# Attention and expert block on one Trainium2 core: TensorE flips after the probability rows, ScalarE moves rows before it copies operands, sine and cosine move to a head's third step

## The chip, the cores and the metric

The kernel runs on one core of a Trainium2 chip, as one launch. The core has TensorE (PE in the profile; PEld is its weight load), VectorE (DVE), ScalarE (ACT), GpSimd (POOL) and the queue that issues transfers (SP). Each engine works through its own instruction stream in order and waits on semaphores for the others. The metric is the device time of one execution in microseconds (us); lower is better.

## What is computed

A transformer block on x of shape (4, 512, 128), float32, with adaptive layer norms. Its first half is an attention with 16 heads of width 64 and 4 key/value heads. Each token picks 2 of 4 nodes for each head; the rotary angle of a token is its rank among the tokens of the same node, so every head of every batch needs sines and cosines of its own. Its second half is a gated feed-forward with 7 experts, a null expert and a shared one. Cut to what matters here:

```python
for n in range(K_NODES):
    p = pos[..., n]                      # rank of the token in node n, per head
    qr = q * cos[p] + rotate_half(q) * sin[p]
    kr = k * cos[p] + rotate_half(k) * sin[p]
    scores = einsum('bhid,bhjd->bhij', qr, kr) * SCALE
    scores = where(causal & member[..., n], scores, NEG)
    outs.append(einsum('bhij,bhjd->bhid', softmax(scores), v))
y = (weights of the two picked nodes * their outs).sum()
x = x + ga * (y @ wo)
x = x + gb * (top-1 expert + shared expert)(layernorm(x))
```

## The kernel before

The change lies in the attention stage, which takes the span from about 85 us to about 875 us. It runs over 4 batches x 16 heads = 64 heads (`NH`), and in each head over 4 tiles of 128 query rows (`TB`). One tile of one head is a step k = 4n + s, with n the head and s = 0 to 3 the tile; there are 256 steps (`STEPS`). Causality makes a step wider with s: its scores have (s + 1) x 128 columns. Two score matrices (e = 0, 1) are made in each step, one for each picked node.

The order on each engine is written out by hand, as a loop over k in which each engine handles a different, older or newer step:

- TensorE, step k: `scores(k)` (L1092, matmuls on L1102 to L1104 for each of the two matrices), then `flip(k + 2)` (L1079, three transposes on L1087 and L1089 that put rotated queries and keys on end), then `prob_rows(k - 4)` (L1107, s + 1 transposes on L1113 of the weighted probabilities). In an odd head's third step (s = 2) it adds `values` (L1116, 16 matmuls on L1121), in every fourth head's third step `project_value` (L1031), in a fourth step (s = 3) `project(n + 3)` (L1038).
- ScalarE, step k: `keep_qk(k + 1)` (L510, copies a flip from PSUM to `QK`, L513), `move_pt(k - 5)` (L516, copies transposed probabilities from PSUM to `accT` in `arena`, L522, s + 1 blocks wide), `weigh_a(k - 2)` (L538, L543), `exponentials(k)` (L525, two instructions on L534), and in an odd head's third step `keep_y` (L546, L550), which waits for `values`.
- VectorE, step k: `row_max(k)` (L827 or L832), `weigh_b(k - 3)` (L842), `inverse_sums(k - 1)` (L837), in steps s = 0 and 1 the rotary products of head n + 2 (L816), and a piece of the preparation of angles for the next eight heads.
- GpSimd, step k: the rotary sums and the scaled keys of later heads (`rotate`, L390 to L409), then `coefficients(k - 1)` (L416), which need `inverse_sums(k - 1)`.

PSUM has 8 banks. Banks 0 to 3 hold scores; `scores(k)` waits for the exponentials of step k - 2 or k - 3 (`before_use`). Bank 7 (`psM`) serves projections and values. Banks 4 to 6 are shared in turn by flips and probability rows: the list `turns` says in which order the two take them, and `wait_turn` makes the user of a turn wait until ScalarE has emptied the turn three before it. In the order before, a list of turns in mid-stage reads t(k + 1), pt(k - 5), t(k + 2), pt(k - 4): so `flip(k + 2)` waits for `move_pt(k - 6)`, and `prob_rows(k - 4)` waits for `keep_qk(k + 1)`. `scores(k)` waits for `keep_qk(k)`.

Once in eight heads (`SPAN`), `trigonometry` runs on ScalarE: with the two `preload_act_table` calls around it that is a table load (L556), a sine over 128 x 2048 (L504), a cosine over 128 x 2048 (L505) and a table load back (L506). The tables of sines are double buffered; its angles are ready once the preparation on VectorE is done, at the third step of head n % 8 = 4, and its results are first needed by VectorE's products at the first step of head n % 8 = 6. It stands seven times in the stage's loop, in heads 5, 13, ..., 53, all odd.

Of the kernel before, what the change touches and what calls it, by code (L numbers as in the profile page):

```python
# [18 lines left out]
NH = B * H  # L19
STEPS = NH * TB  # L20
HALF = HD // 2
SPAN = 8
# [15 lines left out]
def block_kernel(nc, x, wq, wk, wv, wr, wo, w_router, w_up, w_gate, w_down, ws_up, ws_gate, ws_down,  # L38
                 c, wmod, inv_freq, out):
    ctx = ExitStack()  # L40
    with ctx:
# [180 lines left out]
        def score_area(k, e):  # L222
            b_, w = places(k), (k % TB + 1) * P
            return bank[b_[0]][:, e * w:(e + 1) * w] if len(b_) == 1 else bank[b_[e]][:, 0:w]
# [7 lines left out]

        turns = [("t", 0), ("t", 1)]
        for k in range(STEPS + 2 * TB):
            if k + 2 < STEPS:
                turns.append(("t", k + 2))
            if 0 <= k - 4 < STEPS:
                turns.append(("pt", k - 4))
        turn_of = {what: i for i, what in enumerate(turns)}

        def turn_bank(what):
            return bank[4 + turn_of[what] % 3]

        def wait_turn(eng, what):

            i = turn_of[what] - 3
            if i >= 0:
                eng.wait_ge(S["t_ev" if turns[i][0] == "t" else "pt_ev"], turns[i][1] + 1)
# [213 lines left out]
        def _(act):  # L462
# [25 lines left out]
            def keep_value(g):  # L488
                act.wait_ge(S["v_mm"], g + 1)
                act.activation(v_b[:, g % 3, :, :].rearrange("p t d -> p (t d)"), psM[:, 0:TB * HD], ACT.Copy  # L490
                               ).then_inc(S["v_ev"], 1)
# [8 lines left out]
            def trigonometry(j):  # L500

                sine, cosine = [trig[:, j % 2, i, :, :, :, :].rearrange("p h t s f -> p (h t s f)") for i in range(2)]
                act.wait_ge(S["ang_abs"], 2 * j + 2)
                act.activation(sine, sine, ACT.Sin).then_inc(S["trig_done"], 1)  # L504
                act.activation(cosine, cosine, ACT.Sin, scale=-1.0, bias=half_pi[:, 0:1]).then_inc(S["trig_done"], 1)  # L505
                act.preload_act_table(ACT.Exp)  # L506
# [3 lines left out]
            def keep_qk(i):  # L510
                n, tb = i // TB, i % TB
                act.wait_ge(S["t_done"], i + 1)
                act.activation(QK[:, n % 2, :, tb * P:(tb + 1) * P], turn_bank(("t", i))[:, 0:3 * P].rearrange("p (j t) -> p j t", j=3),  # L513
                               ACT.Copy).then_inc(S["t_ev"], 1)

            def move_pt(k):  # L516
                n, ib = k // TB, k % TB
                w = ib + 1
                act.wait_ge(S["pt_done"], k + 1)
                if n >= 3:  # L520
                    act.wait_ge(S["pv_done"], (n - 3) // 2 + 1)
                act.activation(accT[:, n % 3, 0:w, ib * P:(ib + 1) * P],  # L522
                               turn_bank(("pt", k))[:, 0:w * P].rearrange("p (j i) -> p j i", j=w), ACT.Copy).then_inc(S["pt_ev"], 1)

            def exponentials(k):  # L525
                w = (k % TB + 1) * P
                if k >= 3:
                    act.wait_ge(S["wa_done"], k - 2)
                if k >= 4:
                    act.wait_ge(S["acc_done"], k - 3)  # L530
                for e in range(2):
                    area = score_area(k, e)
                    act.wait_ge(S["negmax_done"], 2 * k + e + 1)
                    act.activation((expB if e else expA)[:, k % (4 if e else 3), 0:w], area, ACT.Exp,  # L534
                                   bias=negmax[k % 4][:, e:e + 1], accum_out=den[k % 4][:, e:e + 1]
                                   ).then_inc(S["exp_done"], 1)

            def weigh_a(k):  # L538
                w = (k % TB + 1) * P
                if k >= 4:  # L540
                    act.wait_ge(S["pt_done"], k - 3)
                act.wait_ge(S["coef_done"], k + 1)
                act.activation(acc[k % 4][:, 0:w], expA[:, k % 3, 0:w], ACT.Copy, scale=coef[k % 4][:, 0:1]  # L543
                               ).then_inc(S["wa_done"], 1)

            def keep_y(p):  # L546
                act.wait_ge(S["pv_done"], p + 1)
                if p >= PAIRS:
                    act.wait_ge(S["wo_mm"], p // PAIRS)
                act.activation(yT[:, p % PAIRS, :], psM[:, :], ACT.Copy).then_inc(S["y_ev"], 1)  # L550

            keep_qk(0)
            for k in range(STEPS + 2 * TB):
                n, s = k // TB, k % TB
                if s == 0 and n % SPAN == 5 and n // SPAN + 1 < NH // SPAN:
                    act.preload_act_table(ACT.Sin)  # L556
                    trigonometry(n // SPAN + 1)
                if k + 1 < STEPS:
                    keep_qk(k + 1)
                if 0 <= k - 5 < STEPS:  # L560
                    move_pt(k - 5)
                if 0 <= k - 2 < STEPS:
                    weigh_a(k - 2)
                if k < STEPS:
                    exponentials(k)
                if s == 2 and n % 2 == 1 and n >= 3:
                    keep_y((n - 3) // 2)
                if s == 2 and n % GROUP == 0 and n // GROUP + 1 < B * KV:
                    keep_value(n // GROUP + 1)
# [428 lines left out]
        def _(pe):  # L998
# [32 lines left out]
            def project_value(g):  # L1031
                b = g // KV
                for tb in range(TB):
                    mm_ = pe.matmul(psM[:, tb * HD:(tb + 1) * HD], hT[:, b * T + tb * P:b * T + (tb + 1) * P],
                                    w_v[:, (g % KV) * HD:(g % KV + 1) * HD], start=True, stop=True)
                mm_.then_inc(S["v_mm"], 1)
# [55 lines left out]
            def scores(k):  # L1092
                n, s = k // TB, k % TB
                u, r, w = n % 2, n % RING, (s + 1) * P
                rows = slice(s * P, w)
                pe.wait_ge(S["t_ev"], k + 1)
                pe.wait_ge(S[f"mm_in{r}"], 16 * (n // RING + 1))
                if before_use[k] is not None:
                    pe.wait_ge(S["exp_done"], 2 * before_use[k] + 2)
                for e in range(2):  # L1100
                    o = score_area(k, e)
                    pe.matmul(o, QK[:, u, e, rows], QK[:, u, 2, 0:w], start=True, stop=False)  # L1102
                    pe.matmul(o, mring[:, r, 1 + e, rows], mring[:, r, 0, 0:w], start=False, stop=False)  # L1103
                    pe.matmul(o[:, s * P:w], identbig[:, :], causal[:, :], start=False, stop=True  # L1104
                              ).then_inc(S["scores_done"], 1)

            def prob_rows(k):  # L1107
                ib = k % TB
                pe.wait_ge(S["acc_done"], k + 1)
                wait_turn(pe, ("pt", k))  # L1110
                psPT = turn_bank(("pt", k))
                for jb in range(ib + 1):
                    mm_ = pe.transpose(psPT[:, jb * P:(jb + 1) * P], acc[k % 4][:, jb * P:(jb + 1) * P], ident[:, :])  # L1113
                mm_.then_inc(S["pt_done"], 1)
# [31 lines left out]
            for k in range(STEPS + 2 * TB):  # L1146
                n, s = k // TB, k % TB
                if k < STEPS:
                    scores(k)
                if k + 2 < STEPS:  # L1150
                    flip(k + 2)
                if 0 <= k - 4 < STEPS:
                    prob_rows(k - 4)
                if k == STEPS + 1:
                    pe.wait_ge(S["exp_done"], 2 * STEPS)
                    last_rows(0, PAIRS - 1)
                if s == 2 and n % 2 == 1 and n >= 3:
                    values((n - 3) // 2)
                if s == 2 and n % GROUP == 0 and n // GROUP + 1 < B * KV:
                    pe.wait_ge(S["prod_done"], 4 * (n + 3))  # L1160
                    project_value(n // GROUP + 1)
                if s == 2 and n % H == 2 and n > H:
                    attention_rows(n // H - 1)
                if s == 3 and n + 3 < NH:
                    pe.wait_ge(S["prod_done"], 4 * (n + 3))
                    if n >= 3:
                        pe.wait_ge(S["y_ev"], (n - 1) // 2)
                    pe.wait_ge(S["v_ev"], min(B * KV, n // GROUP + 2))
                    if n % H == 2 and n > H:
                        pe.wait_ge(S["x1_done"], n // H)  # L1170
                    project(n + 3)
# [176 lines left out]
```

## Time and profile before

| | |
|---|---|
| median of 3 runs | 1094.33 us (1090.01 to 1095.94) |
| profiled execution, its own time | 1083.49 us |
| its span in the profile | 1081.7 us |
| mean granted TensorE clock | 0.933 of full speed |
| busy in the span | PE 901.7 us, PEld 624.1, DVE 777.6, ACT 741.4, POOL 616.7 |
| chain that ended last | PE 53%, DVE 24%, ACT 9%, issue 7%, POOL 5%, DMA 1% |

The profile is of one execution. Engines run beside each other, so their busy times don't add up; where an engine sat idle, the profile names what released it. The chain that ended last says which work the end hung on. Durations and waits are read from the timeline, which lists the instructions in order of their start.

### The profile page before, as it was taken

How to read it: one execution, taken by the hardware profiler on the slowest of the kernel's cores; microseconds unless marked ns; L12 is line 12 of the kernel's file. 1: busy time of each engine (PE TensorE's matmuls, PEld its weight loads, DVE VectorE, ACT ScalarE, POOL GpSimd, SP SyncE). 2: the span in 40 equal slices, each digit the busy share in tenths (PEclk: the TensorE clock that was granted, in tenths of full speed). 3: DMA queues.
4: the chain of work that ended last, by engine and by line, in shares of the span. 5: the costliest groups of instructions: out<-in, count | busy, mean ns of one | idle time of the engine just before them, and what ended most of it. 6: DMA issues, size and time to landing. Idle time of an engine off the chain costs nothing.

```text
span 1081.7 us, 19107 instructions
## 1 busy us (share of the span) xinstructions
PE 901.7 (83%) x5907; PEld 624.1 (58%) x5907; DVE 777.6 (72%) x1577; ACT 741.4 (69%) x2017; POOL 616.7 (57%) x872
## 2 busy tenths in 40 slices
PE   3409979997999799879997997999899999697883
PEld 3406646665676566556764665667566666554552
DVE  6887957995887589957785797687867774565443
ACT  3326778778776877888678778875888886544342
POOL 5118757785775577857775787576756660050232
PEclk9559989998999899989998999999989999699997
DMA  9000000100100010000000001010000004112003
GB/s 212 1 1 7 1 21 22 31 22 11 31 22 21 11 32 22 21 21 22 21 22 21 21 22 32 11 32 11 8 2 2 2 4 173 59 34 62 18 21 95
DMA packets 45602, 32.68 MB, mean 30 GB/s; under 512 B 8032, under 2 KB 43488, under 8 KB 45504
## 3 DMA queue, kind: packets, MB, share of 16 engines
q1 hardware_dynamic: 44288, 28.95, 9.4%
q0 software_dynamic: 1216, 2.51, 0.7%
q8 instruction: 51, 0.84, 0.3%
q14 instruction: 47, 0.39, 0.1%
HBM read 18.30 MB, written 12.36 MB: 28 GB/s over the span
## 4 chain that ended last, share of the span: by engine, by line
PE 53%; DVE 24%; ACT 9%; issue 7%; POOL 5%; DMA 1%; ACTq 0%; DVEq 0%; SPq 0%; POOLq 0%
PE psum L1102 17%; PE psum L1121 7%; DVE pcs L816 5%; PE psum L1113 5%; PE psum L1204 5%; POOL R L390 4%; PE psum L1103 4%; PE psum L1041 4%; ACT probs L534 3%; DVE accs L842 3%; PE psum L1087 3%; DVE arena L757 3%; PE psum L1140 2%; DVE negmax L827 2%; PE psum L1104 2%
## 5 line engine op out<-in xcount | busy, mean ns | idle before, releaser
L1102 PE MATMUL psum<-QK 128*128 128x128 f32 (+3 forms) x1024 | 385.1, 462 | 0.1
L534 ACT ACTIVATE probs<-psum,negmax 128x128 f32<-128x128 f32 (+3 forms) x512 | 267.5, 531 | 121.1 <-DVE negmax L832 90.4
L390 POOL TENSOR_TENSOR R<-pcs 128x512 f32<-128x512 f32 x128 | 201.7, 1596 | 73.8 <-DVE pcs L816 73.8
L832 DVE TENSOR_REDUCE negmax<-psum 128x1 f32<-128x384 f32 (+1 forms) x256 | 151.1, 615 | 81.3 <-PE psum L1104 80.0
L416 POOL TENSOR_TENSOR coef<-rden,wslot 128x2 f32<-128x2 f32 x256 | 73.4, 287 | 218.2 <-DVE rden L837 218.2
L1113 PE MATMUL psum<-ident,accs 128*128 128x128 f32 x640 | 117.1, 281 | 72.0 <-ACT QK L513 68.4
L1102 PEld LDWEIGHTS psum<-QK 128*128 128x128 f32 x1024 | 158.5, 195 | 19.1 <-issue 5.3
L842 DVE SCALAR_TENSOR_TENSOR accs<-probs,coef,accs 128x128 f32<-128x128 f32 (+3 forms) x256 | 168.6, 659 | 1.0 <-ACT accs L543 1.0
L543 ACT ACTIVATE accs<-probs,coef 128x128 f32<-128x128 f32 (+3 forms) x256 | 148.8, 581 | 22.3 <-POOL coef L416 13.8
L816 DVE TENSOR_TENSOR pcs<-psum,arena 128x512 f32<-128x512 f32 x256 | 161.8, 673 | 2.8 <-POOL R L390 2.8
L1103 PE MATMUL psum<-mring 128*128 128x128 f16 (+3 forms) x512 | 155.4, 304 | 0.0
L827 DVE TENSOR_REDUCE negmax<-psum 128x2 f32<-128x256 f32 (+1 forms) x128 | 70.7, 552 | 117.4 <-PE psum L1104 116.2
L513 ACT ACTIVATE QK<-psum 128x384 f32<-128x384 f32 x256 | 127.0, 496 | 13.0 <-PE psum L1089 12.8
L1113 PEld LDWEIGHTS psum<-ident,accs 128*128 128x128 f32 x640 | 74.2, 142 | 93.5 <-issue 70.0
L522 ACT ACTIVATE arena<-psum 128x128 f32<-128x128 f32 (+3 forms) x256 | 115.7, 452 | 5.0 <-PE psum L1113 5.0
L1104 PE MATMUL psum<-causal,identbig 128*128 128x128 f16 x512 | 113.6, 222 | 0.0
L1041 PE MATMUL psum<-w_qk,hT 128*128 128x128 f32 x512 | 70.9, 283 | 45.3 <-DVE pcs L816 27.7
L534 ACT ACTIVATION_READ_ACCUMULATOR probs<-psum,negmax 128x1 f32 x512 | 104.8, 205 | 0.0
L1104 PEld LDWEIGHTS psum<-causal,identbig 128*128 128x128 f16 x512 | 51.0, 100 | 90.1 <-issue 75.1
L1087 PE MATMUL psum<-ident,R 128*128 128x128 f32 x512 | 102.3, 282 | 0.0
L1041 PEld LDWEIGHTS psum<-w_qk,hT 128*128 128x128 f32 x512 | 64.6, 198 | 46.7 <-issue 43.3
L1103 PEld LDWEIGHTS psum<-mring 128*128 128x128 f16 x512 | 51.3, 100 | 51.8 <-issue 30.9
(203 smaller groups left out, 1434.5 us busy)
## 6 DMA issues: line engine op xcount, KB each, us to landing
weight_halves<-whl SPq DMA_DIRECT2D x48, 128.0 KB, 2.2
arena<-weight_halves SPq DMA_DIRECT2D x7, 768.0 KB, 7.2
wst<-in_L_ffn_w_up_dram SPq DMA_DIRECT2D x14, 128.0 KB, 2.4
wst<-in_L_ffn_w_gate_dram SPq DMA_DIRECT2D x14, 128.0 KB, 2.4
wst<-in_L_ffn_w_down_dram SPq DMA_DIRECT2D x14, 128.0 KB, 2.5
sorted_rows<-arena SPq DMA_DIRECT2D x1, 1430.0 KB, 11.7
QK<-sorted_rows SPq DMA_DIRECT2D x5, 260.0 KB, 5.0
x<-in_L_attn_x_dram SPq DMA_DIRECT2D x4, 256.0 KB, 4.6
```

The source lines that it names most:

```text
L390: pool.tensor_tensor(R[u][:, :, :, 0:3:2, half * HALF:(half + 1) * HALF].rearrange("p t e j f -> p (t e) j f"), halves(pc, half), halves(p ...
L534: act.activation((expB if e else expA)[:, k % (4 if e else 3), 0:w], area, ACT.Exp, bias=negmax[k % 4][:, e:e + 1], accum_out=den[k % 4][: ...
L543: act.activation(acc[k % 4][:, 0:w], expA[:, k % 3, 0:w], ACT.Copy, scale=coef[k % 4][:, 0:1]).then_inc(S["wa_done"], 1)
L816: dve.tensor_tensor(dst[:, :, e, :].rearrange("p t (j f) -> p t j f", f=HALF), src, table.unsqueeze(2).to_broadcast([P, TB, 4, HALF]), ALU ...
L832: dve.tensor_reduce(negmax[k % 4][:, e:e + 1], score_area(k, e), AX_X, ALU.max, negate=True).then_inc(S["negmax_done"], 1)
L842: dve.scalar_tensor_tensor(acc[k % 4][:, 0:w], expB[:, k % 4, 0:w], coef[k % 4][:, 1:2], acc[k % 4][:, 0:w], ALU.mult, ALU.add).then_inc(S ...
L1041: mm_ = pe.matmul(psM[:, tb * P:(tb + 1) * P], hT[:, b * T + tb * P:b * T + (tb + 1) * P], w_qk[:, h, :, :].rearrange("p j d -> p (j d)"), ...
L1087: pe.transpose(psT[:, e * P:(e + 1) * P], R[u][:, tb, e, 0:2, :].rearrange("p c d -> p (c d)"), ident[:, :])
L1102: pe.matmul(o, QK[:, u, e, rows], QK[:, u, 2, 0:w], start=True, stop=False)
L1103: pe.matmul(o, mring[:, r, 1 + e, rows], mring[:, r, 0, 0:w], start=False, stop=False)
L1104: pe.matmul(o[:, s * P:w], identbig[:, :], causal[:, :], start=False, stop=True).then_inc(S["scores_done"], 1)
L1113: mm_ = pe.transpose(psPT[:, jb * P:(jb + 1) * P], acc[k % 4][:, jb * P:(jb + 1) * P], ident[:, :])
```

## The change

Three orders are changed, and no instruction is added or taken out. TensorE's step becomes scores, probability rows, flips, and the list of turns follows it. ScalarE's step moves rows (`move_pt`) before it copies operands (`keep_qk`). The sine and cosine stand behind these two and behind `weigh_a`, right before `exponentials`, and they do so in the third step of the same head (s == 2) instead of at the top of its first.

```diff
         turns = [("t", 0), ("t", 1)]
         for k in range(STEPS + 2 * TB):
+            if 0 <= k - 4 < STEPS:
+                turns.append(("pt", k - 4))
             if k + 2 < STEPS:
                 turns.append(("t", k + 2))
-            if 0 <= k - 4 < STEPS:
-                turns.append(("pt", k - 4))
...
                 n, s = k // TB, k % TB
-                if s == 0 and n % SPAN == 5 and n // SPAN + 1 < NH // SPAN:
+                if 0 <= k - 5 < STEPS:
+                    move_pt(k - 5)
+                if k + 1 < STEPS:
+                    keep_qk(k + 1)
+                if 0 <= k - 2 < STEPS:
+                    weigh_a(k - 2)
+                if s == 2 and n % SPAN == 5 and n // SPAN + 1 < NH // SPAN:
                     act.preload_act_table(ACT.Sin)
                     trigonometry(n // SPAN + 1)
-                if k + 1 < STEPS:
-                    keep_qk(k + 1)
-                if 0 <= k - 5 < STEPS:
-                    move_pt(k - 5)
-                if 0 <= k - 2 < STEPS:
-                    weigh_a(k - 2)
                 if k < STEPS:
                     exponentials(k)
...
                 if k < STEPS:
                     scores(k)
+                if 0 <= k - 4 < STEPS:
+                    prob_rows(k - 4)
                 if k + 2 < STEPS:
                     flip(k + 2)
-                if 0 <= k - 4 < STEPS:
-                    prob_rows(k - 4)
```

## Rows read from the trace of the kernel before

**Rows 1.** Waits of the whole span: waiter, releaser, total us, times, longest us.
```profile
PE psum L1113 <- ACT QK L513: 68.4, 32, 7.3
```

**Rows 2.** Windows: stretch, length, busy us of PE, PEld, DVE, ACT, POOL, clock, DMA.
```profile
285.00:385.00 100.00, 89.92 (x585) 63.59 (x584) 75.10 (x147) 75.05 (x210) 65.19 (x92) 0.97 0.07 20
355.49:362.69 7.20, 0.00 (x2) 0.03 (x1) 2.33 (x5) 7.14 (x8) 3.29 (x7) 0.78 0.14 39
362.69:366.43 3.74, 3.74 (x14) 2.88 (x15) 0.72 (x2) 2.70 (x9) 0.00 (x0) 0.50 0.02 4
669.90:677.20 7.30, 0.02 (x1) 0.05 (x1) 2.31 (x5) 7.24 (x8) 3.28 (x7) 0.75 0.12 38
952.80:955.30 2.50, 0.09 (x2) 0.02 (x2) 2.33 (x9) 0.00 (x0) 0.45 (x1) 1.00 0.00 0
```

**Rows 3.** Timeline around head 21's sine and cosine: start us, duration us, instruction.
```profile
354.27 0.39 PE L1102 MATMUL psum<-QK 128*128 128x128 f32 x2
...
355.64 1.28 ACT L556 ACT_TABLE_LOAD   x1
...
356.94 1.91 ACT L504 ACTIVATE arena<-arena 128x2048 f32<-128x2048 f32 x1
...
362.05 0.49 ACT L513 ACTIVATE QK<-psum 128x384 f32<-128x384 f32 x1
...
362.69 0.44 PE L1113 MATMUL psum<-ident,accs 128*128 128x128 f32 x1 [7.20 <-ACT QK L513]
...
366.43 0.81 PE L1102 MATMUL psum<-QK 128*128 128x384 f32 x2
```

**Rows 4.** Timeline of head 23, odd and without sine, to head 24's start.
```profile
384.56 0.67 ACT L534 ACTIVATE probs<-psum,negmax 128x512 f32<-128x512 f32 x1
...
385.89 0.48 ACT L513 ACTIVATE QK<-psum 128x384 f32<-128x384 f32 x1
...
386.65 0.66 PE L1102 MATMUL psum<-QK 128*128 128x256 f32 x2
...
387.96 0.39 PE L1087 MATMUL psum<-ident,R 128*128 128x128 f32 x2
...
388.83 0.81 PE L1102 MATMUL psum<-QK 128*128 128x384 f32 x2
...
391.29 0.58 ACT L534 ACTIVATE probs<-psum,negmax 128x384 f32<-128x384 f32 x1 [0.21 <-DVE negmax L832]
...
392.33 0.20 ACT L534 ACTIVATION_READ_ACCUMULATOR probs<-psum,negmax 128x1 f32 x1
...
393.79 0.60 ACT L550 ACTIVATE yT<-psum 128x512 f32<-128x512 f32 x1 [1.27 <-PE psum L1121]
...
394.29 0.48 ACT L513 ACTIVATE QK<-psum 128x384 f32<-128x384 f32 x1
...
394.66 0.50 ACT L522 ACTIVATE arena<-psum 128x384 f32<-128x384 f32 x1
...
396.10 0.39 PE L1087 MATMUL psum<-ident,R 128*128 128x128 f32 x2
...
396.43 0.60 PE L1113 MATMUL psum<-ident,accs 128*128 128x128 f32 x4
...
396.87 1.06 PE L1041 MATMUL psum<-w_qk,hT 128*128 128x128 f32 x8
...
397.76 0.39 PE L1102 MATMUL psum<-QK 128*128 128x128 f32 x2
...
398.48 0.39 PE L1087 MATMUL psum<-ident,R 128*128 128x128 f32 x2
```

**Rows 5.** Timeline, first step of a head that follows an even head.
```profile
512.53 0.53 ACT L513 ACTIVATE QK<-psum 128x384 f32<-128x384 f32 x1
...
512.90 0.65 ACT L522 ACTIVATE arena<-psum 128x512 f32<-128x512 f32 x1
...
513.34 0.66 PE L1102 MATMUL psum<-QK 128*128 128x256 f32 x2
```

## The prediction

> **What bounds the kernel now.** I read the table of busy time, then the windows over the attention stage, then the list of waits, then the timeline around the longest of them. In a window of 100 us in mid-stage TensorE is busy for 90 us and no other engine for more than 75 [rows 2]; so this stage goes at TensorE's pace, and what counts is the tenth in which TensorE stands still. The list of waits names one reason for nearly all of it: `prob_rows` (L1113) waited for `keep_qk` (L513) 32 times, 68.4 us in total, at most 7.3 us [rows 1]. The timeline of TensorE shows seven of these waits at 7.1 to 7.3 us, about 50 us together, once in eight heads; the other 25 share 18 us, 0.3 to 1.7 us each. The reader is to see in rows 3 what the long ones are. In head 21 ScalarE starts its table load at 355.64, right at the top of the first step, and reaches `keep_qk` at 362.05, 6.41 us later. TensorE needs that copy before `prob_rows` may have its turn in PSUM, and it stands from 355.49 to 362.69 [rows 2, 3]. Then it runs at a granted clock of 0.50 (1.2 GHz) for 3.74 us, until 366.43 [rows 2].
>
> The sum is made against the profiled execution, 1083.49 us with a span of 1081.7 us. It lies 10.8 us under the median of the three runs shown; I take the difference that I find from the median, 1094.33 us.
>
> **The change, part one: sine and cosine in the third step.** The burst itself stays as it is, 6.41 us [rows 3]; what changes is what TensorE can still do while it lasts. I follow head 21 with the durations of head 23, which has no burst [rows 4].
>
> *Up to the burst.* ScalarE, free at 355.64, now moves four blocks first and then copies. In rows 5 such a copy occupies ScalarE for 0.37 us before the move starts, and the move takes 0.65 us to its end; the move alone occupies it for about 0.48 us (from the same timeline). So the copy ends at 355.64 + 0.48 + 0.48 = 356.60, and `scores` of the second step starts at 356.65. In head 23 that step's scores take 387.96 - 386.65 = 1.31 us, a flip 396.43 - 396.10 = 0.33 us, and a transpose of probability rows 0.11 us (four in 396.87 - 396.43 = 0.44 us). The second step is thus 1.31 + 0.22 + 0.33 = 1.86 us, and the third begins at 358.5. Today it begins at 366.43 [rows 3]: 7.9 us are gained so far.
>
> *During the burst.* ScalarE needs, from its first item of the first step to the point where it is ready for the third step's exponentials, 391.29 - 0.21 - 385.89 = 5.19 us in head 23 [rows 4]. The burst so starts at 355.64 + 5.19 = 360.8 and ends at 367.2. Queued behind it on ScalarE are both exponentials of the third step, 392.53 - 391.29 = 1.24 us, `keep_y`, 0.50 us (394.29 - 393.79, its `values` are long done by then), and the first item of the fourth step, the move of three blocks, 0.50 us [rows 4]. They end at 367.2 + 1.24 + 0.50 + 0.50 = 369.5. TensorE has all that it needs for the rest of the third step, for `values`, for the fourth step's scores (their bank was emptied by exponentials two steps older, their operand was copied before the burst) and, with the new list of turns, for its probability rows, whose turn waits for a copy made before the burst. In head 23 the stretch from the third step's start to the end of these rows is 396.87 - 388.83 = 8.04 us, with a flip in it that now comes later: 7.71 us [rows 4]. TensorE gets there at 358.5 + 7.7 = 366.2, and then its flip waits for the move until 369.5: a new wait of 3.3 us. VectorE and GpSimd wait behind the exponentials too (`inverse_sums`, `coefficients` and, behind those in GpSimd's queue, the last parts of `rotate` for head 23). By my count these parts end some 2 us before TensorE's first flip of that head, so they cost nothing; without that cover they would add up to 2 us per burst.
>
> *After the burst.* Flip 0.33, `project` 397.76 - 396.87 = 0.89, next head's first scores 398.48 - 397.76 = 0.72 and one transpose 0.11 [rows 4] bring TensorE to 371.55. ScalarE has to do, from 369.35 on (the move lets it go a little before its result has landed), a copy 0.37, `weigh_a` 0.50, the fourth step's exponentials 385.89 - 384.56 = 1.33 and a move of four blocks 0.6 [rows 4, 5]: 372.1. The next flip waits 0.5 us, and with the copy behind that the next scores start 0.6 us later than they would have. After that ScalarE has caught up.
>
> Sum per burst: 7.9 - 3.3 - 0.6 = 4.0 us, times seven 28 us.
>
> What the slow clock costs is inside the first term, since 366.43 is where TensorE really was. The sum supposes that the new wait leaves the clock alone. In the wait from 355.49 the granted clock averaged 0.78 over 7.2 us; with two levels, 1.2 and 2.4 GHz, that is 2 x 0.22 x 7.2 = 3.2 us at the lower, so it fell 4.0 us after TensorE had stopped. In the earliest case (from 669.9, 0.75 over 7.3 us) it fell 3.65 us after. Over an idle stretch of 2.5 us it stayed at 1.00 [rows 2]. The new wait, 3.3 us, lies between, nearer to the 3.65; I take "no fall" and keep the other end for the range.
>
> The burst's length is read off the trace: the load takes 1.28 us and the sine starts at 356.94, 0.02 us behind it [rows 3]. The Trainium skill, "ScalarE: Activation LUTs", section "What ACT_TABLE_LOAD costs", says that every switch of tables costs about 2.66 us, a load of 1.28 us and a drain of 1.38 us. The trace does not agree with the second half. By that rule the burst would be 2.8 us longer, the new wait about 6 us, the clock would fall, and the sum would be about 22 us instead of 28.
>
> **Part two: the two orders.** No work is added, and on ScalarE copy and move swap places, so that `weigh_a` and the exponentials stand where they stood. The moved operations issue no transfers, and SP's queue is not touched. Before, `prob_rows` waited for ScalarE's first item of the same step; now `flip` does, and the copy that the next scores need is ScalarE's second item. Where ScalarE is late, the copy comes a move later. In rows 5, a head behind an even one, the copy would now end at 512.53 + 0.48 + 0.48 = 513.5, and the scores that started at 513.34 start 0.2 us later. One step on, the move is a single block (0.16 us), TensorE no longer waits for a whole copy before its transposes, and by the same count the next scores start 0.1 us earlier than today; the delay is given back. In heads behind odd ones ScalarE is ahead by more than this. In a third step `values` or the long scores cover it, in a fourth `project`. The 25 short waits [rows 1] are set by VectorE's and GpSimd's lateness and stay, some 0.2 us shorter, some longer. I take zero for this part. Its bounds: a gain of at most the 18 us in those waits, of which I expect no more than 5; a loss of 0.2 us in each of 64 heads if nothing is given back, 13 us.
>
> Forecast: 1094.3 - 28 = 1066 us for the median, and about 1055 us for an execution like the profiled one. A change under 0.5% (5.5 us) can't be told from none with this kernel.
>
> **The rivals.**
>
> *The clock falls in the new wait as well.* Against it stands the margin of 0.35 us above, for it that my 3.3 us may be off by as much. Then flip, `project` and scores (1.9 us at full clock) take up to twice as long, of which the 0.6 us of ScalarE's lateness hide a part: about 1.2 us per burst, 8 us in all, and with waits lengthened by as much again 1078 us. The Trainium skill, "TensorE: Matmul & The Clock Gate", section "HAM oscillation", describes a kernel whose clock drops anew in each recurring pause; the seven drops before bear that out for pauses of 7 us. Chance 0.2.
>
> *The wait shrinks further.* If ScalarE reaches the burst earlier, as in heads whose first step isn't delayed by GpSimd's late coefficients (here 1.0 us from 355.55 to 356.65), or if the short waits shrink by 5 us, the gain is 5 us per burst: 1057 us. Chance 0.17.
>
> *The wait only changes its place.* If something that TensorE needs in third and fourth step hung on the exponentials behind the burst (a bank of scores, the turn of `prob_rows`), it would stop some 2.5 to 5 us earlier, and no more than 1 us per burst would be left: 1090 us. The order of turns and banks in the code speaks against it. Chance 0.08.
>
> *Slower: the copy behind the move.* If ScalarE ran late in most steps, each copy would hold the next scores for the length of a move, 0.16 to 0.5 us, 0.3 us on average. It would eat the gain from 28 / 256 = 0.11 us per step on; at 0.15 us in each step it gives 38 us against 28, 1104 us. Against it: the step-by-step reading above finds the delay in one step of a head at most, and only 32 of 256 waits for this copy show at all [rows 1]. Chance 0.07.
>
> My own case has 0.48, with a range of 1060 to 1074. From 1056 to 1083 the four cases on that side are covered but for the tails. Faster by over 0.5%: 0.48 + 0.2 + 0.17, and a little of the third, 0.87; within 0.5%: 0.07; slower: 0.06.
>
> **What the next profile would show.** The waits of L1113 for L513 fall from 68 us to under 20. In their place L1087 waits for L522 (`move_pt`), seven times 3 to 4 us. The table load stands between L543 and L534 of a third step. In the windows behind the burst the clock reads 1.00. The stage ends about 28 us earlier, and the part behind it is as long as before. I would be wrong if the seven waits were still over 5 us, if the clock fell in them, or if a new crowd of waits of 0.1 to 0.4 us on L1102 for L513 appeared in the first steps.

## The result

| | median, us | runs | lowest to highest |
|---|---|---|---|
| before | 1095.13 | 4 | 1090.01 to 1096.98 |
| changed | 1081.11 | 4 | 1076.12 to 1082.15 |

The ratio is 0.987, with a 95% interval of 0.9825 to 0.9916: 14 us less, between 9 and 19. Faster was right, but the gain is half of the 28 us that the sum gave: 1081.11 us lies outside the 1060 to 1074 us of the prediction's own case, and inside the 1056 to 1083 us only with its rivals.

The profiled execution took 1081.21 us, with a span of 1079.4 us and a mean granted clock of 0.945. Set beside the profile before it shows only 2.3 us of gain. The two parts of the span have to be taken apart for that. From head 0's first scores to head 61's first scores ("the stage" in all that follows) the starts of L1102 in the timeline give 875.86 - 84.82 = 791.0 us before and 865.66 - 86.52 = 779.1 us now: 11.9 us less. From there to the end it took 205.8 us before and 213.7 us now; that is looked at last.

The list of waits, changed kernel (waiter, releaser, total us, times, longest us). It answers to [rows 1]:

```profile
PE psum L1087 <- ACT arena L522: 40.1, 44, 3.3
...
PE psum L1113 <- DVE accs L842: 11.9, 22, 1.3
```

The 68.4 us in which `prob_rows` waited for the copy are gone. The flips (L1087) wait for the move instead, and the rows a little for VectorE. The seven waits behind the bursts, 3.1 to 3.3 us each, are 22 of the 40.1 us; the other 37 are short. The timeline of head 21's third and fourth step, changed kernel, answers to [rows 3, 4]:

```profile
359.84 1.28 ACT L562 ACT_TABLE_LOAD   x1
...
361.14 1.91 ACT L504 ACTIVATE arena<-arena 128x2048 f32<-128x2048 f32 x1
...
364.81 0.60 PE L1113 MATMUL psum<-ident,accs 128*128 128x128 f32 x4
...
366.25 0.58 ACT L534 ACTIVATE probs<-psum,negmax 128x384 f32<-128x384 f32 x1
...
367.38 0.59 ACT L550 ACTIVATE yT<-psum 128x512 f32<-128x512 f32 x1
...
367.86 0.50 ACT L522 ACTIVATE arena<-psum 128x384 f32<-128x384 f32 x1
...
368.50 0.66 PE L1087 MATMUL psum<-ident,R 128*128 128x128 f32 x2 [3.09 <-ACT arena L522]
```

The reader is to see the predicted order: burst, exponentials, `keep_y`, the move, and behind it TensorE's flip, which has waited 3.09 us (3.3 were forecast). The flip takes 0.66 us here, where two such transposes took 0.39 us in [rows 4]. Windows of the changed kernel around that wait, and around the same wait in head 13 (columns as in [rows 2]; the number before the DMA share is the granted clock):

```profile
365.41:368.50 3.09, 0.00 (x1) 0.03 (x1) 0.72 (x3) 3.08 (x8) 0.73 (x2) 0.89 0.00 0
368.50:370.88 2.38, 2.38 (x12) 2.38 (x13) 0.00 (x0) 2.38 (x8) 0.04 (x1) 0.50 0.00 0
...
260.00:263.08 3.08, 0.00 (x0) 0.03 (x1) 0.70 (x3) 3.07 (x8) 0.73 (x2) 1.00 0.01 3
263.08:264.40 1.32, 1.31 (x12) 1.32 (x13) 0.00 (x0) 1.32 (x5) 0.04 (x1) 1.00 0.00 0
```

In head 21 the clock fell during the wait (a mean of 0.89 over 3.09 us, where full clock is 2.4 GHz: 2 x 0.11 x 3.09 = 0.7 us at 1.2 GHz, so it fell 2.4 us after TensorE had stopped) and the flip and projection behind it took 2.38 us. In head 13, after a wait of the same length, the same work took 1.32 us at full clock.

Head by head, from one head's first scores to the next head's (worked out from the starts of L1102 in the timelines; us):

```
                      before       changed
heads 5, 13, ... 53   20.9 - 21.6  17.7 16.6 17.8 17.7 17.8 16.7 17.7   sum of 7: -25.7
the heads behind      9.7          11.1 10.0  9.8 10.2 11.2 10.0 11.2   sum of 7:  +5.7
heads 3, 11, 27, 43   14.2         15.9 15.9 16.0 15.8                  sum of 4:  +6.8
the other 43          518.9        520.2                                           +1.3
```

The bursts give 25.7 - 5.7 = 20.0 us. The third line was not in the forecast at all. These four heads had one wait of 1.72 us in their first step, at full clock; now TensorE waits twice there, 1.27 us for VectorE and 0.67 us for ScalarE's move, with 0.33 us of work between. In head 3 the clock still reads 1.00 over both waits, and 0.51 behind them. Windows of head 3, changed kernel, from the first scores on, well into the second step:

```profile
118.73:120.89 2.16, 0.89 (x10) 0.69 (x8) 2.16 (x6) 1.50 (x4) 1.96 (x2) 1.00 0.00 0
120.89:122.00 1.11, 0.43 (x2) 0.27 (x3) 1.11 (x4) 1.11 (x4) 0.90 (x2) 1.00 0.00 0
122.00:124.00 2.00, 2.00 (x8) 1.57 (x9) 1.44 (x4) 2.00 (x9) 1.50 (x3) 0.51 0.00 0
```

and of the kernel before, up to the end of its single wait and behind it:

```profile
116.97:119.90 2.93, 1.23 (x13) 0.98 (x12) 2.93 (x8) 2.27 (x7) 2.63 (x4) 1.00 0.00 0
119.92:122.00 2.08, 1.96 (x13) 1.44 (x13) 2.00 (x5) 2.08 (x9) 1.56 (x4) 1.00 0.00 0
```

Theory: both losses, some 9 us at the bursts and most of the 7 us in the four heads, are the clock's, which falls in or right behind waits that I had held to be too short. Rival: ScalarE is late behind the burst, by more than I counted, and the clock only runs along with it.

### The profile page after: what moved, and what is told of

It is laid out like the page before. It is cut to its first block, busy times and chain, and to the rows that moved or that the text cites. A ratio compares the mean times of both kernels' runs of the same rounds, so it can differ in the third digit from the quotient of the medians.

```text
span 1079.4 us, 19107 instructions
## 1 busy us (share of the span) xinstructions
PE 909.8 (84%) x5907; PEld 636.4 (59%) x5907; DVE 786.2 (73%) x1577; ACT 741.3 (69%) x2017; POOL 613.8 (57%) x872
## 4 chain that ended last, share of the span: by engine, by line
PE 47%; DVE 24%; ACT 14%; issue 7%; POOL 6%; DMA 1%; another core or an unknown queue 1%; ACTq 0%; DVEq 0%; SPq 0%; POOLq 0%
PE psum L1102 14%; PE psum L1204 6%; DVE pcs L816 6%; PE psum L1121 5%; ACT probs L534 5%; POOL R L390 5%; PE psum L1087 3%; DVE accs L842 3%; PE psum L1041 3%; PE psum L1103 3%; DVE arena L757 3%; PE psum L1113 2%; DVE negmax L827 2%; PE psum L1140 2%; ACT arena L522 2%
## 5 line engine op out<-in xcount | busy, mean ns | idle before, releaser
L1102 PE MATMUL psum<-QK 128*128 128x128 f32 (+3 forms) x1024 | 386.4, 463 | 0.1
L842 DVE SCALAR_TENSOR_TENSOR accs<-probs,coef,accs 128x128 f32<-128x128 f32 (+3 forms) x256 | 176.2, 688 | 1.0 <-ACT accs L543 1.0
L1102 PEld LDWEIGHTS psum<-QK 128*128 128x128 f32 x1024 | 159.9, 197 | 19.5 <-issue 5.5
L513 ACT ACTIVATE QK<-psum 128x384 f32<-128x384 f32 x256 | 129.3, 505 | 13.0 <-PE psum L1089 12.8
L1087 PE MATMUL psum<-ident,R 128*128 128x128 f32 x512 | 104.0, 286 | 40.1 <-ACT arena L522 40.1
L1113 PE MATMUL psum<-ident,accs 128*128 128x128 f32 x640 | 115.5, 279 | 12.2 <-DVE accs L842 11.9
L522 ACT ACTIVATE arena<-psum 128x128 f32<-128x128 f32 (+3 forms) x256 | 113.0, 441 | 5.0 <-PE psum L1113 5.0
L1041 PE MATMUL psum<-w_qk,hT 128*128 128x128 f32 x512 | 75.2, 295 | 45.4 <-DVE pcs L816 27.8
L1041 PEld LDWEIGHTS psum<-w_qk,hT 128*128 128x128 f32 x512 | 68.9, 209 | 46.9 <-issue 43.4
L1087 PEld LDWEIGHTS psum<-ident,R 128*128 128x128 f32 x512 | 60.5, 145 | 53.5 <-issue 48.8
L1113 PEld LDWEIGHTS psum<-ident,accs 128*128 128x128 f32 x640 | 69.8, 143 | 29.2 <-DVE accs L842 18.0
```

The source lines that it names most:

```text
L842: dve.scalar_tensor_tensor(acc[k % 4][:, 0:w], expB[:, k % 4, 0:w], coef[k % 4][:, 1:2], acc[k % 4][:, 0:w], ALU.mult, ALU.add).then_inc(S ...
L1041: mm_ = pe.matmul(psM[:, tb * P:(tb + 1) * P], hT[:, b * T + tb * P:b * T + (tb + 1) * P], w_qk[:, h, :, :].rearrange("p j d -> p (j d)"), ...
L1087: pe.transpose(psT[:, e * P:(e + 1) * P], R[u][:, tb, e, 0:2, :].rearrange("p c d -> p (c d)"), ident[:, :])
```

## The experiments

All numbers of the stage below are measured as above, in each kernel's profile. Here they are together (us):

```
kernel                            stage  bursts (sum of 7)  heads behind  3, 11, 27, 43  other 43
before                            791.0  147.7              67.7          56.8           518.9
before, once more                 791.7  148.0              67.7          56.7           519.3
changed                           779.1  122.0              73.4          63.6           520.2
changed, once more                772.3  119.8              69.8          61.0           521.9
sine and cosine alone             771.2  121.6              73.3          56.7           519.5
orders alone                      798.8  154.6              67.2          57.7           519.3
changed, wait filled              771.2  117.1              70.4          60.8           522.9
changed, half sines               757.3  104.6              70.1          60.8           521.9
sine alone, wait filled           759.2  115.4              69.2          56.8           517.8
sine alone, filled more           758.1  115.3              69.1          56.8           516.9
copies ahead                      759.3  107.1              79.0          56.7           516.5
sine alone, behind exponentials   774.3  124.3              73.6          56.7           519.6
sine and TensorE's order          789.6  123.2              74.6          60.8           530.9
sine and ScalarE's order          786.5  123.4              73.3          59.9           529.9
```

**Sine and cosine alone.** The kernel before, with this edit on ScalarE:

```diff
-                if s == 0 and n % SPAN == 5 and n // SPAN + 1 < NH // SPAN:
-                    act.preload_act_table(ACT.Sin)
-                    trigonometry(n // SPAN + 1)
...
                     weigh_a(k - 2)
+                if s == 2 and n % SPAN == 5 and n // SPAN + 1 < NH // SPAN:
+                    act.preload_act_table(ACT.Sin)
+                    trigonometry(n // SPAN + 1)
```

> The old orders of TensorE, ScalarE and turns, with only the sine and cosine moved to the third step. I measure the stage from head 0's first scores to head 61's first scores: 791.0 us before, 779.1 us after. Clock theory (the swapped orders split one wait of 1.7 us in heads 3, 11, 27 and 43 into two, and the clock falls there, which costs 7 us of the stage): these four heads read as before, the seven burst heads gain as in the changed kernel, and the stage takes about 771 us, 8 us less than with the whole change; ratio to before 0.98. Rival (the orders are harmless, and all of the missing gain is ScalarE's lateness behind the burst): the stage takes 779 us, as with the whole change.

Measured: stage 771.2 us; 1074.53 us median, ratio 0.9781 (0.9758 to 0.9804). Heads 3, 11, 27 and 43 are back at 14.2 us, with their single wait of 1.72 us and a clock of 1.00. TensorE's wait behind the burst is 3.16 us (now `prob_rows` for the copy), and the clock fell again in all seven: during the wait in heads 21, 29 and 53, and 0.1 to 1.2 us behind it in heads 5, 13, 37 and 45. Windows of head 21, and of head 5 from its wait's end, where the clock still held, to the next head's first scores (2 x 0.10 x 1.48 = 0.3 us at 1.2 GHz, so it fell 1.2 us behind the wait):

```profile
361.60:364.76 3.16, 0.00 (x1) 0.03 (x1) 0.81 (x3) 3.15 (x8) 0.74 (x2) 0.97 0.00 0
364.76:367.34 2.58, 2.58 (x12) 2.58 (x13) 0.00 (x0) 2.58 (x8) 0.03 (x1) 0.50 0.00 0
...
158.60:160.08 1.48, 1.48 (x12) 1.48 (x13) 0.00 (x0) 1.48 (x5) 0.04 (x1) 0.90 0.04 11
```

Head 5 itself then took 16.6 us, as if nothing had happened; the head behind it, at the lower clock, took 10.9 us, against 9.9 us with the wait filled, below. So the move of the sine is the whole gain, and the orders take from it: this ratio and the 0.987 of the whole change have intervals that don't overlap.

**Orders alone.** The changed kernel with the sine back at the top of the first step.

> The new orders alone; sine and cosine stay at the top of the first step. Clock theory: the stage takes 8 us more than before, 799 us; of these, 7 us in heads 3, 11, 27 and 43, with a granted clock under 1.00 there. Rival (orders harmless): 791 us, within 2.

Measured: stage 798.8 us, one execution, 1101.09 us. The total is as forecast, the place is not. The four heads took 14.3 to 14.5 us, with the same two waits of 1.26 and 0.68 us and a clock of 1.00 behind them. Windows of head 3 behind the second wait, and of head 13, from the end of its 7.06 us wait to where the clock is full again:

```profile
119.10:121.10 2.00, 2.00 (x16) 1.68 (x16) 1.63 (x5) 2.00 (x9) 1.50 (x3) 1.00 0.00 0
...
252.36:258.52 6.16, 6.16 (x21) 4.34 (x22) 2.50 (x6) 4.51 (x16) 0.37 (x2) 0.50 0.00 0
```

The loss lies in the burst heads, 6.9 us in seven, and most of it is the clock's too. Behind head 13's wait TensorE ran 6.16 us at 0.50 here, and 3.76 us in the kernel before (253.41 to 257.17), though the wait itself is no longer (7.06 and 7.20 us). Over the seven it ran 35.1 us at the lower clock, against 25.9 us before (added up from the trace); 9.2 us more at half speed are 4.6 of the 6.9 us. What the other 2.3 us are is not shown. So the swapped orders by themselves cost these four heads 0.1 to 0.3 us each, and the other 1.4 us come and go with the clock: alike waits let it fall in one kernel and not in another.

**Wait filled.** The changed kernel; in `prob_rows` of the seven steps ahead of the wait:

```diff
-                for jb in range(ib + 1):
+                again = 4 if ib == 3 and (k // TB + 1) % SPAN == 5 and (k // TB + 1) // SPAN + 1 < NH // SPAN else 1
+                for jb in list(range(ib + 1)) * again:
                     mm_ = pe.transpose(psPT[:, jb * P:(jb + 1) * P], acc[k % 4][:, jb * P:(jb + 1) * P], ident[:, :])
```

> The whole change, and before the new wait TensorE repeats the four transposes of the probability rows three more times (12 extra transposes, 1.3 us, same data to the same place), in seven steps. Clock theory: the idle time falls from 3.1 to 1.8 us, the clock stays at 1.00 in all seven, and the five bursts that lost the clock each get some 2 us back: the stage takes about 769 us against 779. Rival (ScalarE's lateness sets the pace behind the burst): the wait ends at the same time and nothing is won, 779 us.

Measured: stage 771.2 us, 8 us less than without the extra work; 1072.3 us median, ratio 0.9776 (0.9735 to 0.9817). The wait ended where it did before, with 1.78 us of it idle, and what follows ran at full clock in six of seven (in the last, behind 1.98 us of idle time, it did not). The extra transposes do nothing but keep TensorE busy: what they win is the clock's. This speaks against the rival. The 8 us, though, are against the first profile of the changed kernel; against its second one, below, where fewer bursts lost the clock, they are 1.1 us. The medians stand for the gain (ratio 0.9776 against 0.987, with intervals just apart), and "sine alone, wait filled" below is the firmer proof.

**Half sines.** The changed kernel with the loop's sines and cosines on half of their columns (the other half of each table stays as it was, so this kernel leaves out part of the computation):

```diff
-                act.activation(sine, sine, ACT.Sin)
+                act.activation(sine[:, 0:1024] if j else sine, sine[:, 0:1024] if j else sine, ACT.Sin)
```

> The whole change, and the seven sines and cosines in the loop work on 1024 instead of 2048 columns (the other half stays without its sine and cosine), so the burst is 1.7 us shorter. Both theories: seven times 1.7 us less, 767 us. Clock theory on top of that: the wait of 1.4 us leaves the clock alone, another 10 us, 757 us.

Measured: stage 757.3 us, wait 1.39 us, clock 1.00 behind it in all seven (14.9 to 15.0 us each). The burst heads gained 2.5 us each; 1.7 of that is the burst, the rest the clock.

**Sine alone, wait filled**, with the same idea in the old orders: in `flip` of those steps, `for e in list(range(2)) * again` with `again = 7`.

> The old orders, sine and cosine in the third step, and in the seven fourth steps where TensorE then waits 3.16 us, 12 extra transposes (a flip's two repeated six times more, same data to the same place, 1.3 us at full clock) ahead of the wait. Clock theory: the idle time is 1.8 us, the clock stays at 1.00 in all seven, the stage takes 762 us against 771 without the extra transposes; ratio to before 0.97. Rival (the fall of the clock costs nothing net here, ScalarE's lateness hides it): 771 us.

Measured: stage 759.2 us; 1063.61 us median, ratio 0.9692 (0.9652 to 0.9733). All seven burst heads take 16.4 to 16.6 us, all heads behind them 9.9 us. Windows of head 21: the extra work, the idle rest of the wait, what follows:

```profile
358.38:360.04 1.66, 1.66 (x16) 1.42 (x14) 0.95 (x2) 1.65 (x2) 0.00 (x0) 1.00 0.00 0
360.04:361.89 1.85, 0.00 (x1) 0.03 (x1) 0.17 (x1) 1.85 (x7) 0.73 (x2) 1.00 0.00 0
361.89:363.25 1.36, 1.36 (x12) 1.36 (x13) 0.00 (x0) 1.36 (x5) 0.04 (x1) 1.00 0.06 12
```

The reader should hold the last row against the 2.58 us of the same work without the filling. The clock fell in none of the seven, against all seven without the filling. Of the 12 us less in the stage, 10.3 lie in the burst heads and those behind them; and the two ratios, 0.9692 and 0.9781, have intervals that don't overlap.

**Filled more** (`again = 13`).

> The same with 24 extra transposes (2.7 us), idle time 0.5 us. Clock theory: no more to be had, 762 us again, since the wait ends with ScalarE. If more fill still helped, the state of the clock would depend on idle times as short as 1.8 us.

Measured: stage 758.1 us, the burst heads to 0.1 us as above; one execution, 1062.00 us. The rest of the wait is ScalarE's.

**Copies ahead.** The old orders, and on ScalarE:

```diff
                 if s == 2 and n % SPAN == 5 and n // SPAN + 1 < NH // SPAN:
+                    keep_qk(k + 2)
                     act.preload_act_table(ACT.Sin)
                     trigonometry(n // SPAN + 1)
+                    keep_y((n - 3) // 2)
```

with the same two left out where they stood.

> The old orders, sine and cosine in the third step, but the copy that TensorE's probability rows wait for is made ahead of the sine, and the copy of y that TensorE's projection waits for right behind the cosine, ahead of the exponentials. If the single wait is what costs, seven times 2 us or more are won: 757 us or less. If ScalarE's lateness costs (6.4 us of work that it has to catch up), TensorE gets through the rows and the projection and then waits for the exponentials and the next copies in several short waits, 3 us in all: the wait is only dealt out, and what is won is the clock, 762 to 766 us.

Measured: stage 759.3 us; 1060.17 us median, ratio 0.9705 (0.9663 to 0.9746). Burst heads 15.3 us, 1.2 less than with the wait filled; heads behind them 11.2 us (once 11.6), 1.3 more. The wait is dealt out: in head 21 and the step behind it 1.74 us ahead of `project` and 1.20 us ahead of the rows. The clock stayed up in six of seven. In head 29 it fell 1.7 us behind a wait of 1.73 us (it reads 0.50 from 459.91 to 463.32), and this is the head with 11.6 us behind it. So of what the burst still costs, about 3 us are ScalarE's own lateness, and no order of these instructions got rid of them.

**Behind the exponentials.** The old orders, sine and cosine between `exponentials` and `keep_y`.

> The old orders, sine and cosine behind the third step's exponentials instead of ahead of them. They start 1.2 to 1.5 us later and have 1.24 us less queued behind them: the wait of TensorE is as long as with them ahead, 3.2 us within 0.4, and the stage takes 771 us within 3. If instead the exponentials behind the sine had delayed VectorE and GpSimd to a price, the stage would be 5 us shorter or more.

Measured: stage 774.3 us, wait 3.49 us; one execution, 1081.51 us. The wait is as forecast and the stage 0.3 us beyond the 3 us allowed; the clock fell in or behind all seven waits. There is no sign of the 5 us that VectorE and GpSimd would have had to cost by waiting behind the burst for the exponentials.

**One order alone.** Sine and cosine in the third step in both.

> Sine and cosine in the third step, TensorE's order and the turns swapped, ScalarE's order as before. Heads 3, 11, 27 and 43: the rows wait 1.3 us for VectorE and the flips then 1.1 us for the move, two waits around 0.1 us of work. If it is TensorE's order that lets the clock fall there, some or all of the four heads take 15.9 us instead of 14.2; the stage takes 779 to 785 us.

> Sine and cosine in the third step, ScalarE's order swapped, TensorE's order and the turns as before. The flips fill the start of the wait, so that heads 3, 11, 27 and 43 have one wait, 0.4 us longer than 1.7 us since the copy comes behind the move: 14.6 us each if the clock holds, 16 us if a wait of 2.1 us is enough to let it fall. In first steps of late heads 0.4 us more are lost than with both orders swapped. The stage takes 771 to 781 us.

Measured: 789.6 and 786.5 us; one execution each, 1081.85 and 1078.67 us. Both are worse than I expected, and not in the places I named: the 43 other heads took 530.9 and 529.9 us instead of 519.5. With both orders swapped, TensorE's flips wait for ScalarE's first item; with one swapped, they or the rows wait for the second, in every head where ScalarE is a little late. The two swaps belong together, and together they come to 520.2 us, no gain over 519.5. With TensorE's order alone the four heads had two waits, 0.9 and 1.05 us, and the clock fell behind them in two (15.9 us against 14.5). With ScalarE's order alone they had one wait of 1.8 us, and the clock fell behind it in two (15.6 and 15.8 us against 14.2), as in head 3:

```profile
121.20:122.99 1.79, 0.00 (x0) 0.03 (x1) 1.79 (x7) 1.79 (x7) 1.11 (x3) 1.00 0.00 0
122.99:125.00 2.01, 2.01 (x7) 1.49 (x8) 1.16 (x2) 2.01 (x8) 1.50 (x3) 0.55 0.00 0
```

**The changed kernel once more.**

> The changed kernel once more. If the fall of the clock hung on the kernel's own timing alone, the same heads would show it as in the first profile (heads 3, 11, 27, 43, and 5, 21, 29, 37, 53, not 13 and 45). If it hangs on something that the kernel doesn't set, other heads will: the stage then differs from 779 us by some us.

Measured: stage 772.3 us, 6.8 us less than in the first profile of the same kernel; 1064.51 us against 1086.18 us of the kernel before beside it. Every wait in it is as long as before, to 0.1 us. But now the clock fell in three of the seven burst heads, 5, 45 and 53, and in 3 and 43 of the four. Head 21, which had lost it:

```profile
362.02:365.11 3.09, 0.01 (x1) 0.04 (x1) 0.71 (x3) 3.08 (x8) 0.74 (x2) 1.00 0.00 0
365.11:366.36 1.25, 1.25 (x12) 1.25 (x13) 0.00 (x0) 1.25 (x5) 0.03 (x1) 1.00 0.00 0
```

This is the clearest pair of the study: same kernel, same head, same wait of 3.09 us; 0.50 and 2.38 us of work behind it in one execution, 1.00 and 1.25 us in the other (the windows end at the next head's first scores in both).

**The kernel before once more.**

> The kernel before once more, for the part behind the stage, which took 205.8 us from head 61's first scores to the end in the first profile and 210 to 219 us in all nine others. If the first profile was an exception, it takes about 216 us now, and the stage 791 us.

Measured: stage 791.7 us, and 205.9 us behind it; 1084.16 us. My expectation of 216 us was wrong. The part behind the stage took 204 to 206 us in four of these profiles (the two kernels once more, and each order alone) and in the first profile of before, and 210 to 219 us in the other nine profiles, whatever the kernel. In each of those nine the list of waits or the timeline has pauses of ScalarE in the shared expert's part that are put down to nothing in the kernel (`remote`); the changed kernel's:

```profile
ACT probs L603 <- remote: 7.9, 1, 7.9
```

None of the five short ones has such a line. What the pauses are I can't say; they belong to an execution or a chip, not to the change.

## Why the prediction was right in direction and wrong in size

*What bounds the kernel, and how a burst's cost shrinks:* right. Where the clock held (heads 13 and 45 in the first profile), a burst head and the one behind it take 16.6 + 10.0 us instead of about 21.1 + 9.7: 4.2 us gained, 4.0 forecast. The three terms, measured in head 21: the third step's scores start at 357.33 - 353.13 = 4.2 us after the head's first scores instead of 12.16, 8.0 us (7.9 forecast); the new wait takes 3.09 us (3.3); ScalarE's lateness makes the next head's first step, where the clock held, 1.72 us instead of 1.17 (head 14): 0.55 us (0.6 forecast).

*The step that failed* is the choice of "no fall": the clock's price behind the new wait was put at nothing. It rested on two readings: the clock fell 3.65 us or more after TensorE had stopped in the seven long waits, and stayed up over 2.5 us of idleness. From seven cases I made a threshold. With the change it fell 2.4 us after the stop in head 21, and in, or 0.1 us behind, waits of 3.1 to 3.3 us in five of seven cases in one profile and three of seven in the other. "If the clock fell in them" was one of the prediction's own signs of being wrong. So the bursts gave 20.0 us instead of the 29 us that seven times 4.2 would be, some 9 us lost. The rival in which the clock falls named the mechanism and, with 8 us, about its size; it had a chance of 0.2.

*The second step that failed:* "The 25 short waits ... stay", and "I take zero for this part". As argued, the late heads lost in the first step and got most of it back in the second, but 0.4 and 0.3 us where I had counted 0.2 and 0.1; the 43 other heads lost 1.3 us in all. What I had not looked at was what stood between the waits. In heads 3, 11, 27 and 43 the old order put the flips' work ahead of one wait, the new order puts a first wait right behind the scores and a second one 0.3 us of work later. In the second wait or up to 1.3 us behind it the clock fell in all four (6.8 us), where it did not fall behind 1.72 us in any of the 28 such heads in the seven profiles with both old orders. In five profiles with both new orders it fell in 10 of 20.

The terms together: 28 forecast, less 8.0 at the bursts, less 6.8 and 1.3, is 11.9 us, the stage's gain in the first profile. In the second it is 791.7 - 772.3 = 19.4 us. The medians' 14 us lie between.

*The other rivals:* "the copy behind the move" showed in one step of late heads and was given back in the next, as argued; with one order alone it would have been real (10 us in the 43 heads). "The wait only changes its place" was wrong: TensorE did all the work up to the flip. The Trainium skill, "TensorE: Matmul & The Clock Gate", section "HAM oscillation", says that a kernel which pauses again and again pays the fall anew each time. The trace agrees with it in eight of fourteen bursts, and the filled waits show that it is the pause that is paid for. The Trainium skill, "ScalarE: Activation LUTs", section "What ACT_TABLE_LOAD costs", has a drain of 1.38 us with each load; here too the sine starts 0.02 us behind the load (359.84 + 1.28 to 361.14), so the measurement decides against it, and the fall did not need the longer burst.

*Two sums of the prediction* are a little off, and nothing hangs on them: 28 us less 8 and 8 again gives 1082 us, not 1078; seven times 5 us off 1094.3 us gives 1059 us, not 1057.

*Left open:* why the clock falls in one of two alike waits. The pattern changes between two executions of one kernel, so it isn't the kernel's own timing alone.

## What to carry to other kernels

A long block of work on one engine costs least where the others have the most left to do before they need that engine again; count that work from the program's order, as here, and the wait that remains comes out well: 3.3 us forecast, 3.1 to 3.3 us measured. On TensorE a wait then has a second price, the clock behind it. It need not show in the wait's own window: here the clock fell as late as 1.7 us after TensorE had started again, so the work behind the wait has to be looked at too. And it is not safe to read a length from a few cases up to which it is free: count it with a chance. If a wait of 2 to 3 us can't be removed, useless work in front of it (12 repeated transposes, seven times) was worth 12 us of 771 here with the old orders, and splitting it was worth as much; two orders that belong together shouldn't be judged, or made, one at a time.

The best versions keep the old orders, with sine and cosine in the third step and either the filled wait (1063.61 us, ratio 0.9692) or the copies ahead (1060.17 us, 0.9705). Their intervals overlap; both beat both kernels of this case.

## What the runs showed of the hardware

- The granted clock (0.50 instead of 1.00) fell in, or up to 1.2 us behind, single waits of 3.1 to 3.3 us in 15 of 21 cases (both profiles of the changed kernel, sine and cosine alone), and waits of 3.4 to 3.5 us in 16 of 21 (behind exponentials, and each order alone).
- Of shorter waits, it fell behind one of 1.8 us in 2 of 4 cases (ScalarE's order alone), behind one of 1.74 us in 1 of 7 (copies ahead), behind one of the seven of 1.8 to 2.0 us in the changed kernel with the wait filled, and in none of the seven of 1.85 us with sine alone and the wait filled. Behind 1.72 us it held in 28 of 28.
- It fell in the second of two waits of 1.3 and 0.7 us, or up to 1.3 us behind it, with 0.3 us of work between them, in 10 of 20 (five profiles with both new orders), and behind two of 0.9 and 1.05 us in 2 of 4.
- Two executions of one kernel with the same waits differ in which waits cost the clock: the stage took 779.1 and 772.3 us.
- ScalarE paused for up to 10 us in the part behind the stage in nine of fourteen profiles, with no work of the kernel as the releaser.
